# Scores of a pair's two heads as 64-row tiles on one key buffer; short key tiles share an exponential

## The reference

```
scores = einsum('bhqd,bhkd->bhqk', q, k) / sqrt(dh)        # q, k after rope, dh = 16
scores = where(causal, scores, -inf)
weights = softmax(scores, axis=-1)
out = einsum('bhqk,bhkd->bhqd', weights, v)
```

## Time and profile before

| | |
|---|---|
| median of the runs | 3414.96 us |
| profiled execution, first to last instruction | 3413.7 us |
| one sequence in the attention phase | 145.0 us |
| TensorE busy | 88% of the span |
| VectorE busy | 72% |
| ScalarE busy | 50% |
| GpSimd busy | 22% |

### The profile page before, as it was taken

One profiled execution on the slowest core, in us unless ns is written; L12 is line 12 of the kernel. 1 busy time (PEld: TensorE's weight loads), 2 busy tenths in 40 slices (PEclk: granted clock), 3 DMA queues, 4 the chain that ended last, 5 costly groups with the idle time before them and its releaser, 6 DMA issues. The chain is left out here.

```text
span 3413.7 us, 65137 instructions
## 1 busy us (share of the span) xinstructions
PE 2990.8 (88%) x19840; PEld 1439.9 (42%) x19840; DVE 2466.5 (72%) x7030; ACT 1692.8 (50%) x2220; POOL 759.4 (22%) x918
## 2 busy tenths in 40 slices
PE   3798998988889888888888888897299999999998
PEld 1344444444444444444444444443144444444443
DVE  8778778787887878878788787885655545455554
ACT  1647475574755647566475664755322222222222
POOL 3132332323323223332233322332000000000000
PEclk9999999999999999999999999999599999999999
DMA  2000010000100001000010000000311111111110
GB/s 99 1 13 28 12 38 27 14 26 14 38 27 14 26 14 38 26 14 26 14 38 26 14 26 14 26 26 14 142 38 49 61 49 55 44 51 60 49 61 37
DMA packets 16419, 118.72 MB, mean 35 GB/s; under 512 B 2304, under 2 KB 2304, under 8 KB 2944
## 3 DMA queue, kind: packets, MB, share of 16 engines
q1 hardware_dynamic: 16128, 114.90, 8.9%
HBM read 81.34 MB, written 33.55 MB: 34 GB/s over the span
## 5 line engine op out<-in xcount | busy, mean ns | idle before, releaser
L452 ACT ACTIVATE probs<-ring,exp_scale 128x1024 f32<-128x1024 f32 (+3 forms) x1024 | 811.9, 798 | 339.5 <-PE ring L882 334.5
L641 DVE CUSTOM_DVE_ANT_0 narrow<-narrow,causal 128x384 f32<-128x384 f32 (+3 forms) x1760 | 816.6, 487 | 105.8 <-PE narrow L866 102.1
L866 PE MATMUL narrow<-kTz,qT 128*128 128x384 f16 (+3 forms) x1760 | 502.7, 299 | 158.2 <-DVE row_max L641 126.9
L366 POOL TENSOR_SCALAR_AFFINE_SELECT probs<-probs 128x512 f32<-128x512 f32 x512 | 326.6, 638 | 1361.3 <-ACT probs L452 1360.6
L882 PE MATMUL ring<-qmT,kTz 128*128 128x512 f16 (+3 forms) x2048 | 449.3, 301 | 1.7 <-ACT probs L452 1.0
L1262 DVE SCALAR_TENSOR_TENSOR hidden<-gu,up_scale,silu 128x512 f32<-128x512 f32 x176 | 132.0, 750 | 419.2 <-PE gu L1312 419.2
L1121 ACT ACTIVATE silu<-gu,gate_scale 128x512 f32<-128x512 f32 x176 | 121.0, 688 | 632.2 <-PE gu L1312 632.2
L866 PEld LDWEIGHTS narrow<-kTz,qT 128*128 128x128 f16 x1760 | 170.8, 97 | 545.8 <-DVE row_max L641 459.4
L896 PE MATMUL av<-probs,vs 128*32 128x512 f32 (+3 forms) x4096 | 379.3, 445 | 1.4 <-ACT oT L457 0.6
L1310 PE MATMUL gu<-f_xT_hi,gate_hi 128*128 128x512 f16 x704 | 267.9, 381 | 52.1 <-issue 52.1
L641 DVE DVE_READ_ACCUMULATOR2_ANT row_max<- 128x1 f32 x2048 | 284.7, 139 | 0.0
(11 more groups left out here) (159 smaller groups left out, 5225.7 us busy)
## 6 DMA issues: line engine op xcount, KB each, us to landing
xn<-x SPq DMA_DIRECT2D x16, 1024.0 KB, 4.8
xr<-x SPq DMA_DIRECT2D x16, 1024.0 KB, 4.8
x<-xr SPq DMA_DIRECT2D x16, 1024.0 KB, 3.9
f_xn<-x SPq DMA_DIRECT2D x16, 1024.0 KB, 4.8
f_xr<-x SPq DMA_DIRECT2D x16, 1024.0 KB, 4.8
out<-f_xr SPq DMA_DIRECT2D x16, 1024.0 KB, 3.9
raw_gate<-gateT SPq DMA_DIRECT2D x1, 2816.0 KB, 10.9
raw_up<-upT SPq DMA_DIRECT2D x1, 2816.0 KB, 17.4
```

Of the source, the lines that this page charges most:

```text
L366: nc.gpsimd.affine_select(out=d, in_=d, compare_op=ALU.is_ge, fill=0.0, base=0, pattern=[[0, HG], [1, P]], channel_multiplier=-1).then_inc ...
L452: nc.scalar.activation(probs[:, kt, 2 * pair:2 * pair + 2, P * kt:T], transposed_scores_at(w), ACT.Exp, scale=exp_scale[:, 0:1]).then_inc( ...
L641: nc.vector.tensor_tensor_reduce(out=bank[:, 0:n], in0=bank[:, 0:n], in1=causal[:, T - n:T], scale=1.0, scalar=-3e38, op0=ALU.add, op1=ALU ...
L866: nc.tensor.matmul(bank_of_maximum(2 * s + j)[:, 0:P * (qt + 1)], qT[:, g % 2, pair, P * qt:P * (qt + 1)], kTz[j][:, g % 3, pair, 0:P * (q ...
```

## The change

The two zero-padded key buffers become one, `kT`, that holds both heads. The score matmuls read only the 64 rows of their head (`rows = slice(SLOT * j, SLOT * (j + 1))`), in both `score` and `score_transposed`. ACT copies the transposed k in one piece of 128 rows; the DVE copy is gone. `score_transposed` is called once per head, head 1 first. The last four units of a group (key tiles 2 and 3) no longer have an exponential each: two units fill two ring banks side by side, and one exponential reads both, so a group has 6 exponentials (`NE`) and not 8, of 1024, 1024, 768, 768, 1024 and 512 elements per partition. Ring banks are used in turns of two, and none is spare: `score` has the two `narrow` banks alone. `weigh` moves from even to odd slots (`WEIGH_LAG` 5).

```diff
-        kTz = [sb(f"kTz{j}", [P, 3, 2, T], F16) for j in range(2)]
+        kT = sb("kT", [P, 3, 2, T], F16)
...
-        WEIGH_LAG = 6
+        WEIGH_LAG = 5
+        WEIGHED_LATE = [n for n in range(NG * NT) if 2 * n + WEIGH_LAG >= NS]
...
-            return n if n >= 0 and w % 2 == 0 and n < NG * NT else None
+            return n if n >= 0 and w % 2 == 1 and n < NG * NT else None
...
-            spare = ["spare"] if g >= 0 and u >= 4 else []
-            bank = min(["narrow 0", "narrow 1"] + spare, key=lambda b: last_use.get(b, -3))
...
+        EXPONENTIAL_OF_UNIT = (0, 1, 2, 3, 4, 4, 5, 5)
+        NE = 6
+        EXPONENTIALS_OF_KEYS = (2, 4, 5, 6)
...
+        def maximum_bank(s, j):
+            return narrow[:, j, :]
...
+        def transposed_scores_of(u, j):
+            n = T - P * (u // 2)
+            bank = 2 * (EXPONENTIAL_OF_UNIT[u] % 2) + j
+            at = n * (u % 2) if u >= NT else 0
+            return ring[:, bank, at:at + n]
...
-                if kind == "k":
-                    dst, src = kTz[1][SLOT:P, g % 3, :, :], turn16[SLOT:P]
+                if kind == "k":
+                    dst = kT[:, g % 3, :, :]
...
-            def read_k(i, g):
-                dve.wait_ge(turn_full, N_TURN * i + turn_uses.index(("k", g)) + 1)
-                nc.vector.tensor_copy(kTz[0][0:SLOT, g % 3, :, :], turn16[0:SLOT]).then_inc(turn_read_dve, 1)
...
+                pe.wait_ge(narrow_free, N_NARROW * i + FRONT + 2 * (s - 1) + j + 1)
+                nc.tensor.matmul(maximum_bank(s, j)[:, 0:P * (qt + 1)], qT[rows, g % 2, pair, P * qt:P * (qt + 1)],
+                                 kT[rows, g % 3, pair, 0:P * (qt + 1)], start=True, stop=True).then_inc(narrow_full, 1)
...
-                        score_transposed(i, w)
+                        score_transposed(i, w, 1)
+                        score_transposed(i, w, 0)
```

More of the change, by code:

```diff
@@ L258, in unit_of_maximum, with ends_exponential @@
             return g, QT_OF_UNIT[u], u % 2
[L262 to L272, removed]
-            spare = ["spare"] if g >= 0 and u >= 4 else []
-            bank = min(["narrow 0", "narrow 1"] + spare, key=lambda b: last_use.get(b, -3))
[L275 to L292, removed]
+        EXPONENTIAL_OF_UNIT = (0, 1, 2, 3, 4, 4, 5, 5)
+        NE = 6
+        EXPONENTIALS_OF_KEYS = (2, 4, 5, 6)
+        def ends_exponential(u):
+            return u == NU - 1 or EXPONENTIAL_OF_UNIT[u + 1] != EXPONENTIAL_OF_UNIT[u]
+        def maximum_bank(s, j):
+            return narrow[:, j, :]
+        def transposed_scores_of(u, j):
             n = T - P * (u // 2)
-            if 2 * n <= T:
-                return ring[:, ST_BANK[u], 0:2 * n].rearrange("p (j n) -> p j n", j=2)
-            return ring[:, ST_BANK[u]:ST_BANK[u] + 2, 0:n]
+            bank = 2 * (EXPONENTIAL_OF_UNIT[u] % 2) + j
+            at = n * (u % 2) if u >= NT else 0
+            return ring[:, bank, at:at + n]
         block = ctx.enter_context(nc.Block())
@@ L855, in score @@
                 g, qt, pair = unit_of_maximum(s)
+                rows = slice(SLOT * j, SLOT * (j + 1))
                 if s % NU == 0 and j == 0:
@@ L859, in score @@
                     pe.wait_ge(turn_read_act, BY_ACT * i + read_by("qmk", placed))
[L860 to L866, removed]
-                                 kTz[j][:, g % 3, pair, 0:P * (qt + 1)], start=True, stop=True).then_inc(narrow_full, 1)
@@ L869, in score_transposed @@
[L869 removed]
+                pe.wait_ge(narrow_free, N_NARROW * i + FRONT + 2 * (s - 1) + j + 1)
+                nc.tensor.matmul(maximum_bank(s, j)[:, 0:P * (qt + 1)], qT[rows, g % 2, pair, P * qt:P * (qt + 1)],
+                                 kT[rows, g % 3, pair, 0:P * (qt + 1)], start=True, stop=True).then_inc(narrow_full, 1)
+            def score_transposed(i, w, j):
                 g, u = divmod(w, NU)
                 kt, pair = divmod(u, 2)
[L873 to L885 removed]
@@ new lines, in score_transposed @@
+                rows = slice(SLOT * j, SLOT * (j + 1))
+                e = EXPONENTIAL_OF_UNIT[u]
+                if j == 1:
+                    if u == 0:
+                        pe.wait_ge(turn_read_act, BY_ACT * i + read_by("qmk", turn_uses.index(("m", g)) + 1))
+                    if w < 2:
+                        pe.wait_ge(v_read, NT * i + 2 * w + 2)
+                    else:
+                        pe.wait_ge(st_read, NE * (NG * i + g) + e - 1)
+                scored = nc.tensor.matmul(transposed_scores_of(u, j), kT[rows, g % 3, pair, P * kt:P * (kt + 1)],
+                                          qmT[rows, g % 2, pair, P * kt:T], start=True, stop=True)
@@ L887, in weigh @@
+                if j == 0 and ends_exponential(u):
+                    scored.then_inc(st_full, 1)
             def weigh(i, n):
```

61 lines of the change are left out of this document (25 added, 36 removed).

## The result

The changed kernel takes 3796.3 us (median of 4 runs, 3787.53 to 3802.37), the kernel before 3412.17 us beside it. The ratio is 1.1121, 95% interval 1.1094 to 1.1148: slower by 384 us. The sign was forecast, the size was not (3595, range to 3675).

What follows compares the result with a forecast made beforehand. Inner groups were taken as paced by VectorE and what feeds it, outer stretches by TensorE. Terms 8.4 + 1.5 + 0.2 + 1.0 + 0.7 = 11.8 us a sequence, times 15.5, gave +183: about 3595 us, range 3450 to 3675.

Steps and rivals of the forecast that it cites:

- The stalls: Groups 2 to 5: VectorE waits for scores behind `weigh` and transpositions, 1.8 to 2.4 us a group, +8.4 us a sequence.
- 1.64 was charged: Slot 3, first maximum to the next slot's: 1.64 us with form changes and no row-tile overlap, 1.16 before.
- +1.5: Groups 0 and 1 together: copy of k saved (-0.6 each), stalls on top, net 0.75 each taken.
- VectorE's copy: VectorE's copy of k, 0.61 us: its removal worth -0.6 in groups 0 and 1 each, nothing in groups 2 to 5.
- the stalls of slots 7 and 3: Slot 7 stalls 0.8 us, only 0.1 to 0.4 in groups 0 and 1; slot 3 goes from 1.16 to 1.64.
- The rival with a worse end (3750): A slot's four 64-row matmuls each wait for the one before to drain, 0.2 us each: 3750 us, chance 0.07.
- form changes of +1.0: 13 slots beside the projections: 0.20 us for a way in and out less 0.13 overlap each, about +1.0 us a sequence.
- the sign that I gave: If the 32 us stretch at a sequence's end changes by more than 2.6 us, the row tiles' price is wrong.
- +0.7: The 13 slots before slot 0, two scores each, where TensorE has some air: row tiles cost +0.7 us a sequence.
- The two exponentials fewer: ScalarE, two of 8 exponentials gone, about 0.2 us fixed time each; ScalarE had room in the group, so worth 0.
- The rival "TensorE is what binds": VectorE never waits; copies count in full (4.8 us), row tiles overlap free (3.4 us): -127, 3288 us, chance 0.09.

## Why the prediction was wrong

**The stalls were right.** For groups 2 to 5 the sum had +8.4 us a sequence. At full clock, 128 rows, the run with the changed order has 12.75, 14.00, 12.71 and 14.01 (1267.89 to 1321.36) against 10.47, 12.18, 10.47 and 12.28: +8.1. In the clean group of the changed kernel the slots agree to 0.04 us but for one: slot 3 took 1.45 us where 1.64 was charged, and the terms listed for it add to 1.51. The small misses are in groups 0 and 1: 12.69 and 14.31 against 10.86 and 12.32, +3.8 where I had +1.5 (this run keeps VectorE's copy, worth up to 0.6 in each by the prediction). I had let the stalls of slots 7 and 3 vanish in part behind VectorE's other work there; the sum of the two groups suggests that little of them did, but I did not follow it slot by slot.

**The step that failed is the sum itself: it has no term for TensorE's clock.** It went by durations at the clock of one sequence of the trace before, 1.00 in every group, and asked of the row tiles only whether they overlap and what a form change costs. With 64-row tiles the clock falls, most in groups 0 and 1 (before and just after `weigh` begins) and in group 5, and with it nearly doubles the very `weigh` and transpositions that hold up the scores. That two tiles side by side leave TensorE, which already stands idle in many slots, with less to stream would explain it, but no run separates this from a form that counts for less. The forecast had +183 us and the runs gave +384; between 128 and 64 rows in the changed order lie 124 of them (3672 to 3796), about 8 us a sequence. Adding matmuls raised the clock and cut the time in two kernels, by 33 us each. The price stood in the trace before, in group 0 of another sequence than the one that I read, where the clock had fallen with 128-row matmuls (mean clock 0.72):

```profile
405.36:417.58 12.22, 10.60 (x65) 5.79 (x65) 11.00 (x46) 9.18 (x11) 3.31 (x5) 0.72 0.00 1
```

The same group takes 10.86 us at 1.00. The rival with a worse end (3750) had serial drains as its mechanism, and those did not happen.

**A second term was missed.** I moved `weigh` kt 0 to slot 5 and looked only at its mask; I did not check its other wait, for ScalarE's read of `av` in the same slot. In the changed kernel that is two long waits (3.2 us a sequence) in a stretch where I had charged form changes of +1.0: removing it gave back 40 us, and 95 with eight exponentials, where ScalarE is also late in the groups. The stretch, 31.99 us before, ends with ScalarE's last copy of q after rope. Here it is in the changed kernel (twice), in the same order with 128 rows, and in the even order with 64 and with 128 rows:

```profile
1399.65:1433.07 33.42, 29.73 (x180) 12.78 (x178) 25.94 (x40) 16.11 (x18) 18.93 (x20) 1.00 0.01 1
1230.05:1265.14 35.09, 31.40 (x180) 13.21 (x178) 25.94 (x40) 16.12 (x18) 18.93 (x20) 0.95 0.01 1
...
1335.39:1368.73 33.34, 29.61 (x180) 13.65 (x178) 25.83 (x40) 16.11 (x18) 18.94 (x20) 1.00 0.01 1
...
1268.82:1300.80 31.98, 30.41 (x188) 13.05 (x187) 26.05 (x40) 16.22 (x18) 18.94 (x20) 1.00 0.01 2
...
1258.75:1290.73 31.98, 30.39 (x188) 13.84 (x187) 25.92 (x40) 16.23 (x18) 18.94 (x20) 1.00 0.01 2
```

It changed by 1.4 or by 3.1 us. By the sign that I gave, more than 2.6 would have meant a wrong price of the row tiles; but 128 rows have the same lengths, and with ScalarE's read a slot earlier it is 31.24 us at clock 1.00 in every sequence: it was the wait, and the clock that falls with it. The form changes cost 0.0 to 0.1 us in this stretch, where I had +1.0. Between it and group 0, at full clock and in even slots, 64 rows take 29.6 to 30.2 us and 128 rows 28.6 to 29.1 (all sequences but the first and the last), about 1 us more, where I had +0.7. So the row tiles cost about 1 us a sequence at full clock beside the groups, where I had 1.7.

**The bookkeeping.** Two banks +101, odd slots +163 (95 of it the read), row tiles in the odd order +124 (3672 to 3796): 388, where 384 were measured. The two exponentials fewer bought nothing that can be seen, as predicted. The removed copy of k went with the row tiles in every run, and its own worth is not shown; the two together are 0.05 us in groups 2 and 4 of the changed order (12.66 against 12.71). The rival "TensorE is what binds", with 0.09, is refuted: with row tiles that do overlap, nothing was gained at full clock in the changed order.

What stays open: why 64-row tiles lower the clock, whether the fall in group 5 has the same cause as the one in groups 0 and 1, and whether in group 1 the clock could be held, which was not tried.

## What to carry to other kernels

When an edit makes TensorE's work shorter in a stretch where it already waits, write down the granted clock as a term with both ends: what is on the path at full and at half speed. Read it over all repetitions of the stretch, not over one. Before moving a consumer a slot earlier, list all its waits, not only the one that the move is about; the buffer it overwrites has a reader too. A bank that looks spare may be what lets two in-order engines pass a long block of other work.

## What the runs showed of the hardware

Two 64-row tiles in different rows started in the same instant, and the four matmuls of a slot within 0.22 us. Going over from 128-row transpositions to a 64-row tile cost 0.10 us (0.56 against 0.46); among the projections' matmuls 64 and 128 rows made no difference (31.98 us both). In the changed kernel group 0's mean granted clock was 0.60 with TensorE busy by the records for 77% of it (12.22 of 15.89 us), before it was 1.00 with 77% as well (8.33 of 10.86 us): the busy share does not show the fall, since at the lower clock each record is longer (1.93 for 1.07 us). The clock rose with added matmuls of either form, 128 or 64 rows. The row tiles (with VectorE's copy of k gone) moved the mean clock of the span from 0.971 to 0.907 in the odd order and from 0.969 to 0.928 in the even one.
